# The values of an 8-head attention made in an earlier stage and kept in DRAM, and the heads' product moved one step later

## The chip, the cores and the metric

The kernel runs on one core of a Trainium2 chip. The metric is the device time of one execution in microseconds (us). All data is float32 unless said otherwise.

## The reference, cut to what matters

The input is x (32 batches of 128 tokens, 128 wide) and a context (32 x 128 tokens, 96 wide). Eight sublayers are added to x one after the other, each on a layer norm of x. Two of them matter here. The third pair's attention keeps the 32 highest of 128 scores in each of 4 heads (the "top-32 attention"). The last attention is the "8-head attention":

```python
q = (x @ Wq).reshape(B, Nq, 8, 64)
k = (context @ Wk).reshape(B, Nc, 8, 64)
v = (context @ Wv).reshape(B, Nc, 8, 64)
sim = jnp.einsum('bihd,bjhd->bhij', q, k) * 64 ** -0.5
attn = jax.nn.softmax(sim, axis=-1)
out = jnp.einsum('bhij,bjhd->bihd', attn, v)
return out.reshape(B, Nq, 512) @ Wo + bo
```

Its v depends on the context and on Wv alone, not on x.

## The kernel before, in words

The program is written for the engines by hand, stage after stage, with a barrier between stages. Within a stage each engine has its own list of instructions, in the order in which the loops write them, and semaphores tie the lists together. An instruction that waits holds up all that stands behind it on its engine.

**The film stage** (`film_in`, from about 205 to 480 us) holds the top-32 attention. It goes through the 32 batches in 16 pairs p. For each pair VectorE finds the 32 highest scores in four rounds of `max` (L1581) and `match_replace` (L1587). TensorE makes the scores of pair p+1 (L1373, L1376), turns the weights of pair p-2 (L1389), multiplies them with the context and makes the film product (L1410). ScalarE evacuates the scores from PSUM to SBUF (L1468), takes two sets of exponentials (L1452, L1460) and evacuates the film product (L1475). SP stores half of each batch's film product to DRAM (L1271) and loads the toeplitz matrices of the convolution that follows. Scores use columns 0 to 127 of PSUM banks 0 to 3.

**The 8-head stage** (`fp8_attention8`, from about 905 to 1152 us) runs steps n = -15 to 33. It has to finish two sublayers at once: the fp8 layer before (quantize x, turn it, multiply with the quantized weight, add, L2786) and the 8-head attention. Groups of four batches are prepared steps ahead: norm, turning (L2682), and per step one of the group's K products (L2623) and Q products (L2662), each 512 columns, both through PSUM bank 6. K is evacuated by ScalarE (L2720), Q by VectorE (L2825). From step 27 on no K and Q products are left. Step n then does, in this order on TensorE:

1. scores of batch n+1 (L2613, 16 listed products of two heads side by side);
2. the K product;
3. the output product of batch n-1 (L2632, bank 7), which waits for the copy `oT`;
4. the turning of batch n's weights (L2647, banks 4 and 5), which waits for GpSimd's scaling (L2581);
5. the V product of batch n+1 (L2657, bank 7);
6. the Q product;
7. the heads' product of batch n (L2670, bank 4): turned weights by values;
8. now and then four small transposes or the fp8 product: L2690 (quantized x) in steps with n mod 4 = 0, L2698 (fp8 product, bank 7) with n mod 4 = 1, L2682 (norm) with n mod 4 = 2.

ScalarE: K's evacuation, the exponentials of batch n+1, heads 0 to 3 (L2710), two evacuations of the turned weights of batch n (L2734), the exponentials of heads 4 to 7, then the evacuations and the scaling of x that belong to a group (L2747, L2753, L2759). Each exponential also gives a sum.

VectorE: the fp8 result (L2786, n mod 4 = 2), the maxima of the scores of batch n+1 (L2793), the shift, that is maximum times -1/8 (L2800, a `tensor_tensor` with both inputs in SBUF), x plus output product (L2805), the first half of a quantizing (n mod 4 = 3), the copy of V (L2819), the copy of Q (L2825), the second half of the quantizing, the moments (n mod 4 = 2), the normalizing (L2848, n mod 4 = 1), the reciprocal of the sums of batch n+1 (L2859), and the copy `oT` of the heads' product of batch n (L2864). From step 26 on the norm of the next stage is spread over five steps.

GpSimd: it waits for the reciprocal and scales the weights of batch n in two operations of 128x512 (L2581); after them stand the root of the variance (L2587 and L2589, n mod 4 = 3) and the bias added to x (L2593, n mod 4 = 2).

## Time and profile before

| | us |
|---|---|
| median of 3 runs | 1423.41 |
| lowest and highest | 1423.28 and 1425.81 |
| the profiled execution: its time | 1424.34 |
| its span, first to last instruction | 1422.6 |
| mean granted TensorE clock, share of full | 0.867 |

| engine | busy, us | share of the span |
|---|---|---|
| TensorE (PE) | 1180.1 | 83% |
| VectorE (DVE) | 986.3 | 69% |
| ScalarE (ACT) | 691.7 | 49% |
| GpSimd (POOL) | 548.6 | 39% |

A share is an average over stages with different limits, so the rows further down are read stage by stage. PE is TensorE's products, PEld its weight loads (the stationary operand), which run beside the products. A float32 product is listed as two MATMULs. In a row of the timeline the first number is the start in us from the begin of the span and the second the duration in us; "x4" means that four instructions are merged; the bracket names the idle time of the engine before the row and what ended it.

### The profile page before, as it was taken

Reading aid. Unit: us, or ns where it says so; the run is one execution under the profiler, and the core shown is the slowest. Engines: PE = TensorE matmul, PEld = TensorE weight load, DVE = VectorE, ACT = ScalarE, POOL = GpSimd, SP = SyncE. Lnnn points to the kernel's source line nnn. Section 1 sums busy time; section 2 is a strip of 40 time slices with the busy share of each in tenths; the row PEclk is TensorE's granted clock in tenths of the full one; section 3 lists DMA queues with packets and bytes.
Section 4 is the critical chain, followed back from the end, with each engine's and each line's share of the span. In section 5 each row is a group of like instructions: output and inputs, shape, how many; then the busy total and the mean of one; then the engine's idle time right before and its main releaser. Section 6 shows DMA issues by size and latency. Waiting matters only on the chain. (4 is left out here: it accounts for less than half of the span.)

```text
span 1422.6 us, 30767 instructions
## 1 busy us (share of the span) xinstructions
PE 1180.1 (83%) x10551; PEld 809.0 (57%) x10551; DVE 986.3 (69%) x3891; ACT 691.7 (49%) x2026; POOL 548.6 (39%) x770
## 2 busy tenths in 40 slices
PE   4778664767766758997899999699999989999998
PEld 3534322435444535664677777266667667776776
DVE  6767668999999269976478777676775644444433
ACT  3343245777766244432345454366666643333343
POOL 4576665677764256534133332233333310000000
PEclk8688885866676779998799999699999999898989
DMA  6400104000001411100000000000000000000000
GB/s 171 99 0 1 46 21 123 16 29 21 27 24 45 123 56 42 38 23 30 6 3 3 3 4 3 1 1 1 1 2 1 2 1 1 15 0 15 0 16 15
DMA packets 61249, 36.62 MB, mean 26 GB/s; under 512 B 19477, under 2 KB 58992, under 8 KB 61106
## 3 DMA queue, kind: packets, MB, share of 16 engines
q1 hardware_dynamic: 59802, 34.48, 8.6%
q8 instruction: 79, 1.29, 0.4%
q14 instruction: 64, 0.52, 0.1%
q10 hardware_dynamic: 1304, 0.33, 0.1%
HBM read 25.21 MB, written 6.42 MB: 22 GB/s over the span
## 5 line engine op out<-in xcount | busy, mean ns | idle before, releaser
L3037 DVE SCALAR_TENSOR_TENSOR k_X<-ps,m_gt,k_X 128x128 f32 (+1 forms) x256 | 72.0, 344 | 121.3 <-PE ps L2921 121.3
L2960 ACT ACTIVATE m_hid<-ps,k_b 128x512 f32<-128x512 f32 x128 | 81.8, 684 | 133.8 <-PE ps L2921 127.7
L2921 PEld LDWEIGHTS ps<-k_w,m_hid 128*128 128x128 f32 x1024 | 123.1, 192 | 26.8 <-issue 19.6
L2910 PE MATMUL ps<-m_xnT,k_w 128*128 128x512 f32 x256 | 128.9, 634 | 1.2 <-PEq L72 1.2
L2921 PE MATMUL ps<-k_w,m_hid 128*128 128x128 f32 x1024 | 123.3, 275 | 0.0
L2581 POOL TENSOR_TENSOR l_p<-l_p,l_rsum 128x512 f32<-128x512 f32 x64 | 65.3, 1041 | 142.8 <-DVE l_rsum L2859 142.8
L2289 DVE TENSOR_REDUCE g_peak<-ps 128x8 f32<-128x1024 f32 x64 | 75.4, 1219 | 43.5 <-PE ps L1978 43.5
L2710 ACT ACTIVATE l_p<-ps,l_shift 128x128 f32<-128x128 f32 x256 | 91.6, 391 | 19.8 <-DVE l_shift L2800 15.3
L1587 DVE MATCH_REPLACE8 v_left<-c_top,v_left 128x128 f32<-128x128 f32 x384 | 100.8, 274 | 0.0
L711 PE MATMUL ps<-f_expT,f_xeT 128*128 128x512 f32 x128 | 74.7, 718 | 27.6 <-DVE k_X L1089 27.6
L2184 ACT ACTIVATE g_pT<-ps 128x1024 f32<-128x1024 f32 x64 | 62.0, 1021 | 72.5 <-PE ps L1994 72.5
L1581 DVE MAX8 c_top<-v_left 128x8 f32<-128x128 f32 x384 | 77.9, 274 | 0.0
L121 POOL TENSOR_TENSOR m_rstd<-m_ve,k_half 128x8 f32<-128x8 f32 x4 | 6.6, 1640 | 175.6 <-DVE m_ve L114 175.6
L842 ACT ACTIVATE f_part<-ps,f_wf 128x128 f32<-128x128 f32 x128 | 36.5, 368 | 72.9 <-issue 49.1
L2910 PEld LDWEIGHTS ps<-m_xnT,k_w 128*128 128x128 f32 x256 | 48.0, 206 | 41.6 <-issue 41.6
L1389 PE MATMUL ps<-k_ident,c_exa 128*128 128x128 f32 x256 | 57.0, 414 | 10.7 <-POOL c_exa L1334 10.7
L1389 PEld LDWEIGHTS ps<-k_ident,c_exa 128*128 128x128 f32 x256 | 54.5, 321 | 18.6 <-POOL c_exa L1334 18.6
L711 PEld LDWEIGHTS ps<-f_expT,f_xeT 128*128 128x128 f32 x128 | 25.8, 225 | 65.6 <-DVE k_X L1089 44.8
L1373 PE MATMUL ps<-c_kT,c_qT 32*128 32x128 f32 x256 | 22.1, 426 | 45.3 <-ACT v_sc L1468 42.6
L1089 DVE SCALAR_TENSOR_TENSOR k_X<-ps,f_wf,k_X 128x128 f32<-128x128 f32 x128 | 44.6, 349 | 21.6 <-PE ps L711 17.5
L2710 ACT ACTIVATION_READ_ACCUMULATOR l_p<-ps,l_shift 128x1 f32 x256 | 59.1, 231 | 0.0
L1452 ACT ACTIVATE c_exb<-v_left,c_shift 128x128 f32<-128x128 f32 x128 | 49.6, 391 | 12.2 <-DVE v_left L1587 12.2
(539 smaller groups left out, 3129.9 us busy)
## 6 DMA issues: line engine op xcount, KB each, us to landing
v_toep<-kpad SPq DMA_DIRECT2D x4, 1024.0 KB, 9.2
fo_dram<-c_fo SPq DMA_DIRECT2D x32, 128.0 KB, 1.7
g_v<-fo_dram SPq DMA_DIRECT2D x8, 512.0 KB, 3.5
d_mine<-d_wad SPq DMA_DIRECT2D x32, 96.5 KB, 1.9
k_X<-in_x SPq DMA_DIRECT2D x8, 256.0 KB, 3.4
v_late<-kpad SPq DMA_DIRECT2D x2, 1024.0 KB, 8.7
out<-k_X SPq DMA_DIRECT2D x8, 256.0 KB, 2.4
f_cx<-in_ctx SPq DMA_DIRECT2D x4, 384.0 KB, 5.3
```

The lines of the kernel that those rows point to most:

```text
L711: pe.matmul(ps[:, 4 + (2 * b + h) % 3, :], xeT[:, t % 2, u, cols], expT[:, 4 * h:4 * h + 4, :].rearrange("p e d -> p (e d)"), start=True, ...
L1389: m = pe.matmul(ps[:, 4 + a, 0:128], exa[:, i % 4, h, :], k.ident[:], start=h == 0, stop=h == H - 1)
L1581: dve.max((first if r == 0 else top)[:, a, h, :], (sc if r == 0 else left)[:, i % 4, h, :]).then_inc(top_done, 1)
L1587: dve.match_replace(left[:, i % 4, h, :], (first if r == 0 else top)[:, a, h, :], (sc if r == 0 else left)[:, i % 4, h, :], TAKEN).then_in ...
L2184: act.activation(pT[:, n % 2, 2 * h:2 * h + 2, :].rearrange("p a n -> p (a n)"), ps[:, 4 + 2 * h:6 + 2 * h, :].rearrange("p a n -> p (a n) ...
L2289: dve.tensor_reduce(peak[:, (n + 1) % 2, :].rearrange("p (r c) -> p r c", r=BANDS)[:, 2 * h:2 * h + 2, 0:BANDS], ps[:, 2 * h:2 * h + 2, :] ...
L2581: pool.tensor_tensor(p[:, n % 3, 4 * a:4 * a + 4, :], p[:, n % 3, 4 * a:4 * a + 4, :], rsum[:, n % 3, 4 * a:4 * a + 4].rearrange("p (h o) ...
L2710: act.activation(p[:, i % 3, h, :], ps[:, 2 * (i % 2) + a, 128 * b:128 * b + 128], ACT.Exp, bias=shift[:, i % 2, h:h + 1], scale=SCALE, ac ...
L2910: pe.matmul(ps[:, 4 * u + q, :], k.w1_3[:, e, 128 * q:128 * q + 128], xnT[:, u], start=True, stop=True).then_inc(s["hid_ps"].sem, 1)
L2921: m = pe.matmul(ps[:, 4 * u + 2 + e % 2, j * S:j * S + S], hid[:, u, q, j * S:j * S + S], k.w2_3[:, e, q, :], start=q == 0, stop=q == 1)
L2960: act.activation(hid[:, u, q, :], ps[:, 4 * u + q, :], ACT.Gelu, bias=k.b1_3[:, 2 * e + q:2 * e + q + 1]).then_inc(s["hid"].sem, 1)
L3037: dve.scalar_tensor_tensor(out=xj[u][j], in0=ps[:, 4 * u + 2 + e % 2, j * S:j * S + S], scalar=gt[:, u, j, e:e + 1], in1=xj[u][j], op0=ALU ...
```

## The change

The V products of all batches are made in the film stage, in columns 128 to 255 of PSUM banks 0 to 3, beside the scores. TensorE makes them for batch 2p ahead of the scores of batch 2p+2, and for batch 2p+1 ahead of the scores of batch 2p+3, as four products of 128 columns each. ScalarE evacuates them (`spilled`), the one of batch 2p between the evacuation of the scores of 2p+2 and the exponentials of 2p+1, the one of 2p+1 behind the scores' of 2p+3. SP stores each as 256 KB in DRAM (`keep`). In the 8-head stage SP loads them back, three batches ahead, and the V product and its copy are gone.

In the 8-head stage, three orders change. On TensorE the heads' product of batch n-1 follows the scores of batch n+1 (it was the product of batch n at the end of the step), its result goes to bank 7, and the output product of batch n-1 stands behind the turning of batch n. On VectorE the copy `oT` of batch n-1 stands behind the shift. On ScalarE the evacuation of K stands behind the exponentials of heads 0 to 3.

```diff
@@ film_in, SP @@
+            def keep(i):
+                sp.wait_ge(val_done, i + 1)
+                sp.dma_start(k.v_dram[:, i, :], val[:, i % 2].rearrange("p h c -> p (h c)")).then_inc(k.v_out[i % 2], 16)
+
+            for i in range(4):
+                keep(i)
             for i in range(B):
...
+                if i % 2 and i + 4 < B:
+                    keep(i + 3)
+                    keep(i + 4)
@@ film_in, TensorE @@
+            def values(i):
+
+                pe.wait_ge(sc_done, min(i + 2, B))
+                if i:
+                    pe.wait_ge(val_done, i)
+                for h in range(4):
+                    m = pe.matmul(ps[:, h, 128:256], k.cT[:, S * i:S * i + S], k.wv3[:, 128 * h:128 * h + 128],
+                                  start=True, stop=True)
+                m.then_inc(val_ps, 1)
...
+                if pair(p):
+                    values(2 * p)
                 if pair(p + 1):
                     scores(2 * (p + 1))
...
+                if pair(p):
+                    values(2 * p + 1)
                 if pair(p + 1):
                     scores(2 * (p + 1) + 1)
@@ film_in, ScalarE @@
+            def spilled(i):
+                act.wait_ge(val_ps, i + 1)
+                if i >= 2:
+                    act.wait_ge(k.v_out[i % 2], 16 * (i // 2))
+                act.activation(val[:, i % 2], ps[:, 0:4, 128:256], ACT.Identity).then_inc(val_done, 1)
...
                 if pair(p + 1):
                     scored(2 * (p + 1), p)
                 if pair(p):
+                    spilled(2 * p)
+                if pair(p):
                     whole(2 * p + 1)
                 if pair(p + 1):
                     scored(2 * (p + 1) + 1, p)
+                if pair(p):
+                    spilled(2 * p + 1)
@@ fp8_attention8 @@
+        @block.sync
+        def _(sp):
+            for i in range(B):
+                if i >= 3:
+                    sp.wait_ge(av_ps, i - 2)
+                sp.dma_start(v[:, i % 3], k.v_dram[:, i, :]).then_inc(v_in[i % 3], 16)
@@ TensorE @@
+                if 0 <= n - 1 < B:
+
+                    i = n - 1
+                    pe.wait_ge(pT_done, 2 * n)
+                    pe.wait_ge(v_in[i % 3], 16 * (i // 3 + 1))
+                    pe.wait_ge(x8_done, begun(n - 1, 11))
+                    if i:
+                        pe.wait_ge(x_done, i)
+                    for b in range(4):
+                        for a in range(2):
+                            h = 2 * b + a
+                            m = pe.matmul(ps[DH * a:DH * a + DH, 7, 128 * b:128 * b + 128], v[:, i % 3, DH * h:DH * h + DH],
+                                          pT[:, i % 2, 4 * a + b, :], start=True, stop=True)
+                    m.then_inc(av_ps, 1)
                 g, b = item(n)
...
-                if 0 <= n + 1 < B:
-                    i = n + 1
-                    if n >= 1:
-                        pe.wait_ge(x_done, n)
-                    else:
-                        pe.wait_ge(v_done, i)
-                        pe.wait_ge(x8_done, begun(n - 1, 11))
-                    pe.matmul(ps[:, 7, :], k.cT[:, S * i:S * i + S], k.wv3[:], start=True, stop=True).then_inc(v_ps, 1)
+                if 0 <= n - 1 < B:
+
+                    i = n - 1
+                    pe.wait_ge(oT_done, n)
+                    for b in range(4):
+                        m = pe.matmul(ps[:, 7, 0:128], oT[:, i % 2, b, :], k.wo3[:, b, :], start=b == 0, stop=b == 3)
+                    m.then_inc(out_ps, 1)
...
@@ ScalarE @@
+                if 0 <= n + 1 < B:
+                    act.wait_ge(shift_done, n + 2)
+                    if n >= 2:
+                        act.wait_ge(pT_ps, 2 * (n - 1))
+                    weights(n + 1, 0)
                 g, b = item(n)
                 if g:
                     act.wait_ge(k_ps, 4 * g + b + 1)
                     if g >= 2 and b == 0:
                         act.wait_ge(sc_ps, G * (g - 1))
                     act.activation(kT[:, g % 2, b, :], ps[:, 6, :], ACT.Identity).then_inc(k_done, 1)
-                if 0 <= n + 1 < B:
-                    act.wait_ge(shift_done, n + 2)
-                    if n >= 2:
-                        act.wait_ge(pT_ps, 2 * (n - 1))
-                    weights(n + 1, 0)
@@ VectorE @@
                 if 0 <= n - 1 < B:
                     i = n - 1
-                    dve.wait_ge(out_ps, i + 1)
-                    dve.wait_ge(xb_done, i // G + 1)
-                    dve.scalar_tensor_tensor(out=k.X[:, i, :], in0=ps[:, 7, 0:128], scalar=k.tg[:, 3:4], in1=k.X[:, i, :],
-                                             op0=ALU.mult, op1=ALU.add).then_inc(x_done, 1)
+                    dve.wait_ge(av_ps, n)
+                    if i >= 2:
+                        dve.wait_ge(out_ps, i - 1)
+                    dve.tensor_copy(oT[:, i % 2].rearrange("p a b -> p (a b)"), ps[:, 7, :]).then_inc(oT_done, 1)
...
-                if 0 <= n + 1 < B:
-                    i = n + 1
-                    dve.wait_ge(v_ps, i + 1)
-                    if i >= 2:
-                        dve.wait_ge(av_ps, i - 1)
-                    dve.tensor_copy(v[:, i % 2], ps[:, 7, :]).then_inc(v_done, 1)
+                if 0 <= n - 1 < B:
+                    i = n - 1
+                    dve.wait_ge(out_ps, i + 1)
+                    dve.wait_ge(xb_done, i // G + 1)
+                    dve.scalar_tensor_tensor(out=k.X[:, i, :], in0=ps[:, 7, 0:128], scalar=k.tg[:, 3:4], in1=k.X[:, i, :],
+                                             op0=ALU.mult, op1=ALU.add).then_inc(x_done, 1)
...
-                if 0 <= n < B:
-                    dve.wait_ge(av_ps, n + 1)
-                    if n >= 2:
-                        dve.wait_ge(out_ps, n - 1)
-                    dve.tensor_copy(oT[:, n % 2].rearrange("p a b -> p (a b)"), ps[:, 4, :]).then_inc(oT_done, 1)
```

## Rows read from the trace of the kernel before

**Rows 1.** Busy time by stretch: top-32 attention, 8-head stage, its last steps.

```profile
core 0: us, PE busy (x) PEld busy (x) DVE busy (x) ACT busy (x) POOL busy (x), PEclk, DMA share, GB/s
300.00:360.00 60.00, 42.69 (x217) 27.51 (x216) 60.00 (x403) 43.86 (x178) 42.95 (x76) 0.67 0.08 25
1020.00:1052.00 32.00, 31.29 (x257) 21.78 (x255) 22.91 (x49) 20.78 (x82) 12.66 (x13) 1.00 0.01 2
1116.00:1145.00 29.00, 23.39 (x222) 16.98 (x221) 19.20 (x51) 17.51 (x82) 10.74 (x10) 1.00 0.01 2
```

**Rows 2.** Timeline of the 8-head stage, 1115 to 1125 us (start, duration).

```profile
1115.18 1.02 PE L2657 MATMUL ps<-k_wv,k_cT 96*128 96x512 f32 x2
...
1116.05 1.02 PE L2662 MATMUL ps<-l_xnT,k_wq 128*128 128x512 f32 x2
...
1117.11 0.69 DVE L2825 COPY l_qT<-ps 128x512 f32<-128x512 f32 x1 [0.17 <-PE ps L2662]
...
1118.49 0.18 DVE L2859 RECIPROCAL l_rsum<-l_total 128x8 f32<-128x8 f32 x1
...
1118.76 2.04 POOL L2581 TENSOR_TENSOR l_p<-l_p,l_rsum 128x512 f32<-128x512 f32 x2 [5.07 <-DVE l_rsum L2859]
...
1120.49 0.33 DVE L2800 TENSOR_TENSOR l_shift<-l_top,l_minus 128x8 f32<-128x8 f32 x1
...
1120.86 0.37 ACT L2710 ACTIVATE l_p<-ps,l_shift 128x128 f32<-128x128 f32 x1 [2.87 <-DVE l_shift L2800]
...
1122.24 1.09 ACT L2734 ACTIVATE l_pT<-ps 128x512 f32<-128x512 f32 x2
...
1124.77 0.20 DVE L2859 RECIPROCAL l_rsum<-l_total 128x8 f32<-128x8 f32 x1 [0.89 <-ACT l_p L2710]
```

**Rows 3.** Timeline, the first steps of the 8-head stage.

```profile
922.86 0.60 ACT L2720 ACTIVATE l_kT<-ps 128x512 f32<-128x512 f32 x1 [1.21 <-PE ps L2623]
...
923.35 0.36 ACT L2710 ACTIVATE l_p<-ps,l_shift 128x128 f32<-128x128 f32 x1
923.51 0.30 PEld L2662 LDWEIGHTS ps<-l_xnT,k_wq 128*128 128x128 f32 x2 [0.66 <-ACT l_kT L2720]
...
924.67 0.69 DVE L2825 COPY l_qT<-ps 128x512 f32<-128x512 f32 x1
...
926.60 0.20 DVE L2859 RECIPROCAL l_rsum<-l_total 128x8 f32<-128x8 f32 x1
...
927.92 1.02 DVE L2800 TENSOR_TENSOR l_shift<-l_top,l_minus 128x8 f32<-128x8 f32 x1
...
928.98 0.37 ACT L2710 ACTIVATE l_p<-ps,l_shift 128x128 f32<-128x128 f32 x1 [1.56 <-DVE l_shift L2800]
...
932.53 0.23 PEld L2690 LDWEIGHTS ps<-k_identb,l_xq 128*128 128x128 bf16 x4 [0.17 <-issue]
...
932.86 0.97 PEld L2613 LDWEIGHTS ps<-l_kT,l_qT 64*128 64x128 f32 x16
```

**Rows 4.** Timeline, the last reciprocal of the 8-head stage.

```profile
1143.74 0.20 DVE L2859 RECIPROCAL l_rsum<-l_total 128x8 f32<-128x8 f32 x1 [0.58 <-ACT l_p L2710]
```

**Rows 5.** Timeline, copy of Q and reciprocal in a step with moments.

```profile
1062.33 0.69 DVE L2825 COPY l_qT<-ps 128x512 f32<-128x512 f32 x1 [0.17 <-PE ps L2662]
...
1063.99 0.17 DVE L2859 RECIPROCAL l_rsum<-l_total 128x8 f32<-128x8 f32 x1
```

**Rows 6.** Timeline of the top-32 attention: second scores evacuated, first read.

```profile
364.68 0.58 ACT L1468 ACTIVATE v_sc<-ps 128x512 f32<-128x512 f32 x1
...
372.93 1.25 DVE L1581 MAX8 c_first<-v_sc 128x8 f32<-128x128 f32 x6
```

**Rows 7.** Timeline, GpSimd's root and VectorE's shift at the same time.

```profile
1037.52 1.04 POOL L2589 TENSOR_TENSOR l_rs<-l_rs,k_half 128x4 f32<-128x4 f32 x1
1037.59 0.17 DVE L2800 TENSOR_TENSOR l_shift<-l_top,l_minus 128x8 f32<-128x8 f32 x1
```

**Rows 8.** Timeline, VectorE's shift and GpSimd's bias add.

```profile
1086.78 0.42 DVE L2800 TENSOR_TENSOR l_shift<-l_top,l_minus 128x8 f32<-128x8 f32 x1
...
1087.13 1.27 POOL L2593 TENSOR_TENSOR k_X<-k_X,k_bo 128x512 f32<-128x512 f32 x1
```

More of the change, by code:

```diff
@@ L1187, in stage_film @@
         k.fo_out = [once(f"fo_out{i}") for i in range(2)]
+        k.v_out = [once(f"v_out{i}") for i in range(2)]
         k.sc = ctx.enter_context(nc.sbuf_tensor("v_sc", [128, CH, 128], F32))
@@ L1642, in _ @@
                 sp.wait_ge(k.fo_out[a], 16 * B // 2)
+                sp.wait_ge(k.v_out[a], 16 * B // 2)
         @block.tensor
@@ L2663, in _ @@
                               stop=True).then_inc(q_ps, 1)
[L2664 to L2675 removed]
+                if n == B - 1:
+                    pe.wait_ge(p_done, H * B)
+                    ex.logits(pe, ps, 0, 0)
                 g = due(n, 6)
```

41 lines of the change are left out of this document (13 added, 28 removed).

## The prediction, made before the changed kernel ran

> **What bounds the kernel now.** I read first the busy time by stretch, with the granted clock, then the 8-head stage in order of time. In 32 us of that stage TensorE is busy 31.29 us at a clock of 1.00, VectorE 22.91, ScalarE 20.78, GpSimd 12.66; in its last 29 us, where no K and Q products are left, TensorE is busy only 23.39 us, still at 1.00. In the top-32 attention VectorE is busy 60.00 of 60 us and TensorE and ScalarE 42.69 and 43.86 [rows 1]. So the change takes work from the engine that looks full and gives it to two that wait. The reader should not stop there: there is a second loop in the stage, nearly as long as TensorE's work, and it doesn't contain the product that leaves.
>
> **The second loop.** I cut steps at VectorE's reciprocal of the sums (L2859). In a last step it starts at 1118.49; GpSimd scales the weights from 1118.76 for 2.04 us, to 1120.80; the shift (L2800, VectorE, two inputs in SBUF) ends at 1120.82, and ScalarE's first exponential starts at 1120.86, 2.37 after the reciprocal. The evacuation of the turned weights follows at 1122.24, the next reciprocal at 1124.77, 3.91 after the first exponential: 6.28 in all [rows 2]. The shift waits for GpSimd, not for its maximum. The start of the stage shows it best, since no copy of the heads' product stands there between reciprocal and maximum, as none will after the change: reciprocal 926.60, shift asked for at 927.92, and it takes 1.02 instead of 0.17, so that the exponentials start at 928.98, 2.38 after the reciprocal [rows 3]. Hence the copy of the heads' product (at most the 0.69 of Q's, 1117.11) which the change moves behind the shift was free already: W, from reciprocal to first exponential, stays 2.38.
>
> **The V product** leaves TensorE's queue: 1115.18 to the Q product at 1116.05 is 0.87 a step [rows 2], its copy, 0.69 by Q's, leaves VectorE's. From first to last reciprocal, 926.60 to 1143.74, the 31 steps take 217.14 us, 7.00 each [rows 3, 4]; without V TensorE needs about 6.1 of it. If it were the only bound, 31 x 0.87 = 27 us would go.
>
> **The K evacuation** is moved on ScalarE from before the first four exponentials to behind them. Before, it ran while ScalarE waited for the shift (free). Now it stands inside the loop, between exponentials and turned weights: 922.86 to 923.35, 0.49 to 0.50 of ScalarE [rows 3]. The loop of a plain step with K and Q is 2.38 + 3.91 + 0.49 = 6.78. That is above TensorE's remaining work, so ScalarE, VectorE and GpSimd set the time.
>
> **The Q product** waits for that evacuation. Exponentials take 1120.86 to 1122.24 = 1.38, the evacuation 0.60 to its end; the load for Q follows 0.05 later, and the copy of Q starts 1.16 after that (922.86 + 0.60, 923.51, 924.67) [rows 2, 3]. So VectorE copies Q at W + 3.2 = 5.6. Behind the copy stand the norm or quantizing operations, and only then the reciprocal: 1.66 from the copy's start with moments (1062.33 to 1063.99) [rows 5], taken also for the normalizing; 1.93 with the quantizing (924.67 to 926.60) [rows 3].
>
> **Step lengths after.** A step n scales and turns batch n and takes the scores of n+1. For n mod 4, while groups are left:
> n=0: 6.78, ScalarE sets it. Here the heads' product no longer covers TensorE's wait for the copy of Q (5.6 + 0.69) ahead of the quantized transposes (932.53 to 932.86, 0.33) [rows 3], so the next scores start at 6.6 and their maximum some 1.2 later (0.97 of loads and the end of the last products, an estimate), about 1.05 after the next reciprocal. W of the next step grows by 0.2.
> n=1: 2.59 + 3.19 + 1.66 = 7.44.
> n=2: the product by the values must wait for VectorE's fp8 result (same bank); scores being early, K, turning, output product and Q queue up behind it, and the copy of Q starts 0.1 late (an estimate): 2.38 + 0.1 + 3.19 + 1.66 = 7.33.
> n=3: 2.38 + 3.19 + 1.93 = 7.50.
> The sum: 11 steps without such work 74.6, 5 of 7.44 = 37.2, 5 of 7.33 = 36.6, 4 of 7.50 = 30.0, one with a normalizing alone 7.2, one with the first of the next stage's moments 6.93 (1.38 behind the copy of Q, 1117.11 to 1118.49), and the last four as they are, 25.25 [rows 2, 4]: 217.8 against 217.14, +0.6. The step ahead of the first reciprocal adds more: its exponentials still start at 923.3, but K's evacuation ends at 925.3 instead of 923.46, and Q, its copy and the quantizing behind it shift the first reciprocal from 926.60 to 928.4, +1.8 [rows 3]. Stage: +2.4.
>
> **The top-32 side.** Each batch adds four 96x128 products and a 128x512 evacuation, 0.58 by the one of the scores (364.68). The second batch of a pair has its scores at 365.26 and VectorE asks for them at 372.93: 7.7 us of cover [rows 6]. Per pair ScalarE gets 1.2 us and TensorE about 2 (unknown: from 1.0 to 3, as the clock there is 0.67). Priced at nothing, covered by VectorE's full queue; with no cover it would be up to 16 x 3 = 48. On SP the 32 stores of 256 KB stand before stores that come a pair later, and the toeplitz loads behind them wait for later events anyway; DMA is at 8% there [rows 1]. Nothing. The loads back (three ahead, in the 8-head stage at a DMA share of 0.01) are due two steps, 13 us, after they are issued; 0, and up to +3 if the first are late. Five more semaphores have no row; taken at 0.
> The tail (last reciprocal to the experts) keeps its order share, turn, product, output: 0, between -0.5 and +0.5.
>
> **A rule weighed.** An operation of GpSimd with tiny operands does not hold the shift: L2589 runs from 1037.52 for 1.04 us, and the shift at 1037.59 takes 0.17 [rows 7]. So I charge nothing where it follows the scaling. The Trainium skill, "SBUF — State Buffer", section "SBUF: two separate sides", has GpSimd and VectorE lock their shared ports for a whole instruction, whichever starts first. By that a shift overtaken by L2589 would pay some 1.0 in each n=3 step, 5 us in all; the measured row speaks against it.
>
> **The sum**: profiled execution 1424.34 + 2.4 = 1426.7. That execution is 0.93 above the median, so for the median 1423.41 + 2.4 = **1425.8**. A measurement can tell about 0.2% (2.85 us) from no change.
>
> **Rivals.**
> *Slower, the add overtakes the shift (0.14).* In n=2 steps the bias add on GpSimd (L2593, 1.27) follows the scaling directly. After the change the shift is asked for some 0.3 before the scaling ends. It decides who gets in first. For me: the shift asked for at 1086.78, 0.4 before the scaling's end, ended at 1087.20 although the add is shown from 1087.13 [rows 8]. Against: the margin is small. If the add wins, 5 steps grow by 1.2: 1425.8 + 6 = 1432.
> *Faster, the shift slips between the two halves of the scaling (0.12).* It is asked for at 1.32 to 1.37 after the reciprocal, and the first half ends at about 1.3. At 927.92 it missed [rows 3]. Were it granted there, W falls to about 1.65, the loop to 6.05, nearly TensorE's work: 31 x 0.7, some 22 to 24 us less: 1403. If even K's evacuation were hidden, TensorE alone would bound: 1397.
> *Slower, the top-32 stage pays (0.04)*: ScalarE's 32 x 0.58 on the path: 1444.
> *Slower, TensorE's clock falls (0.03).* It idles about 1 us a step. The last steps idled as much at 1.00 [rows 1]. At the lower level its 6 us would take up to 12: tens of us, 1460 and more. The Trainium skill, "TensorE: Matmul & The Clock Gate", section "A second HAM failure mode: psum-queue depth-cycling", says that frequent small pauses between groups of products make the clock oscillate; by it this rival would hold, the rows at 1.00 do not bear it out.
> That the change does not do what it says: V's product has no other place left, so 0.
>
> **Chances.** The forecast 0.67; its own errors (W of n=1 steps, the queue behind the fp8 result, the first reciprocal) are some 2.5 us, which puts 0.25 above +2.85, 0.02 below -2.85 and 0.40 within. With the rivals: faster 0.14, same 0.40, slower 0.46. The range 1420 to 1432 takes in the add and leaves out the slipped shift, the top-32 cost and the clock. The likeliest case's own range is 1423 to 1429.
>
> **What would show it.** Right: L2657 and L2819 gone from the stage; TensorE near 27 of 32 us; reciprocal to first exponential still 2.38 with a shift of about 1 us; K's evacuation between the fourth exponential and the turned weights; plain steps of 6.78, the last four 6.28; the first reciprocal 1.8 later; VectorE 60 of 60 in the top-32 stretch. Wrong: shifts of 0.17 asked for at 1.37 (faster rival), shifts ending with L2593 (slower), idle time of VectorE before L1581, a clock under 1.00.

## The result, and the profile after

The changed kernel takes **1431.75 us** (median of 7 runs, 1429.21 to 1433.87); the kernel before 1420.81 (7 runs: the three of its table, 1423.28 to 1425.81, and four more, 1418.05 to 1420.81). The ratio is 1.0070, 95% interval 1.0053 to 1.0086: slower, by 7.5 to 12 us. The forecast was 1425.8, with 1420 to 1432 around it; the time lies 0.25 us inside the upper edge of that range and above the likeliest case's own 1423 to 1429: +10.9 us in place of +2.4.

The profiled execution after took 1431.95 us, its span is 1430.2 (1424.34 and 1422.6 before), its mean granted clock 0.882 (0.867). Stage by stage, in us of the two traces:

| stretch | before | after |
|---|---|---|
| film stage: first moments (L1577) to first Toeplitz product (L1692) | 268.6 | 274.0 |
| from there to the first maximum of the 8-head stage | 443.3 | 442.1 |
| first maximum (L2835) to first reciprocal (L2901) | 4.80 | 6.60 |
| first to last reciprocal, 31 steps | 217.1 | 222.7 |
| last reciprocal to the experts | 18.7 | 18.9 |

The rows add up to +11.7 us, while the two traces differ by 7.6: the film stage starts 2.4 us earlier in the trace after (207.4 against 209.9; 205.5 to 209.7 in all kernels with the new film stage, whose code ahead of it is the same), and from the experts on it takes 1.6 less. The stages are therefore compared one by one.

The busy time by stretch, after (the counterpart of [rows 1]; the columns are those there):

```profile
300.00:360.00 60.00, 44.76 (x279) 34.03 (x280) 60.00 (x403) 46.61 (x180) 42.42 (x77) 0.77 0.18 60
1020.00:1052.00 32.00, 28.00 (x248) 19.35 (x244) 20.85 (x46) 19.82 (x83) 11.80 (x13) 1.00 0.14 35
1121.00:1150.00 29.00, 23.96 (x220) 18.23 (x217) 18.93 (x43) 17.09 (x80) 11.78 (x11) 0.94 0.13 37
```

TensorE has fallen from 31.29 to 28.00 of 32 us, and the steps have not become shorter. VectorE still shows 60.00 of 60 us in the top-32 stretch. A plain step of the 8-head stage, after (timeline):

```profile
1120.71 0.20 DVE L2901 RECIPROCAL l_rsum<-l_total 128x8 f32<-128x8 f32 x1 [0.49 <-ACT l_p L2752]
...
1120.99 2.04 POOL L2628 TENSOR_TENSOR l_p<-l_p,l_rsum 128x512 f32<-128x512 f32 x2 [4.73 <-DVE l_rsum L2901]
...
1122.04 1.01 DVE L2842 TENSOR_TENSOR l_shift<-l_top,l_minus 128x8 f32<-128x8 f32 x1
...
1123.09 0.37 ACT L2752 ACTIVATE l_p<-ps,l_shift 128x128 f32<-128x128 f32 x1 [2.41 <-DVE l_shift L2842]
...
1124.47 0.61 ACT L2767 ACTIVATE l_kT<-ps 128x512 f32<-128x512 f32 x1
...
1124.94 1.10 ACT L2776 ACTIVATE l_pT<-ps 128x512 f32<-128x512 f32 x2
```

Reciprocal to first exponential is 2.38, with a shift of 1.01 that ends when the scaling does (1120.99 + 2.04); K's evacuation stands between the exponentials and the turned weights and takes 0.47 of the loop. In [rows 2] the turned weights followed the exponentials directly. Reciprocal to reciprocal is 6.74 to 6.77 in nearly all plain steps with K and Q (forecast 6.78) and 6.27 to 6.28 in the last four (forecast 6.28).

The first steps, TensorE's rows, after:

```profile
923.35 1.12 PE L2684 MATMUL ps<-k_cT,k_wk 96*128 96x512 f32 x2
926.97 1.13 PE L2713 MATMUL ps<-l_xnT,k_wq 128*128 128x512 f32 x2 [2.50 <-ACT l_kT L2767]
...
931.44 0.65 PE L2697 MATMUL ps<-k_ident,l_p 128*128 128x128 f32 x4 [1.19 <-POOL l_p L2628]
932.43 1.05 PE L2697 MATMUL ps<-k_ident,l_p 128*128 128x128 f32 x4 [0.34 <-POOL l_p L2628]
934.48 2.07 PE L2713 MATMUL ps<-l_xnT,k_wq 128*128 128x512 f32 x2 [1.00 <-ACT l_kT L2767]
937.39 0.58 PE L2732 MATMUL ps<-k_identb,l_xq 128*128 128x128 bf16 x4 [0.83 <-issue]
937.90 2.08 PE L2660 MATMUL ps<-l_kT,l_qT 64*128 64x128 f32 x16
```

and the granted clock there, after:

```profile
924.00:932.00 8.00, 4.31 (x26) 1.98 (x24) 5.42 (x10) 3.39 (x17) 1.73 (x3) 1.00 0.00 0
932.00:940.00 8.00, 5.83 (x29) 3.37 (x30) 1.21 (x3) 4.96 (x20) 2.41 (x3) 0.53 0.00 0
940.00:948.00 8.00, 7.35 (x56) 5.36 (x56) 4.36 (x11) 4.47 (x19) 0.02 (x1) 0.83 0.12 33
```

TensorE idles 2.50 us before the Q product of step -1, then 1.19, 0.34 and 1.00, and from 932.5 to 942.8 it is granted 1.2 instead of 2.4 GHz: the Q product takes 2.07 instead of 1.13, the scores 2.08 instead of 1.16. Steps 0 and 1 last 7.13 and 10.51 us where the same kinds last 6.76 and 7.46 later. The clock also falls in the last steps, from 1137.4 to 1140.8 (the 0.94 in the row from 1121 us), there without making a step longer.

### The profile page after: what moved, and what is told of

Its sections match the earlier page's. It is cut to its first block and busy times, and to the rows that moved or that the text cites. A ratio compares the mean times of both kernels' runs of the same rounds, so it can differ in the third digit from the quotient of the medians.

```text
span 1430.2 us, 31244 instructions
## 1 busy us (share of the span) xinstructions
PE 1176.1 (82%) x10743; PEld 829.3 (58%) x10743; DVE 973.8 (68%) x3859; ACT 706.6 (49%) x2058; POOL 549.0 (38%) x770
## 3 DMA queue, kind: packets, MB, share of 16 engines
q8 instruction: 81, 1.33, 0.4%
## 5 line engine op out<-in xcount | busy, mean ns | idle before, releaser
L711 PE MATMUL ps<-f_expT,f_xeT 128*128 128x512 f32 x128 | 70.9, 684 | 29.3 <-DVE k_X L1089 29.0
L1398 PE MATMUL ps<-k_wv,k_cT 96*128 96x128 f32 x256 | 48.0, 348 | 52.6 <-ACT c_val L1502 52.6
L1398 PEld LDWEIGHTS ps<-k_wv,k_cT 96*128 96x128 f32 x256 | 42.6, 252 | 66.1 <-ACT v_sc L1496 62.5
L1942 POOL TENSOR_TENSOR g_mq<-g_qT,g_hmask 128x512 f32<-128x512 f32 x32 | 33.2, 1039 | 56.0 <-ACT g_qT L2242 36.8
L1488 ACT ACTIVATE c_exa<-v_sc,c_shift 128x128 f32<-128x128 f32 x128 | 49.7, 398 | 5.4 <-POOL c_shift L1320 5.4
```

Source lines behind the costliest of these rows:

```text
L711: pe.matmul(ps[:, 4 + (2 * b + h) % 3, :], xeT[:, t % 2, u, cols], expT[:, 4 * h:4 * h + 4, :].rearrange("p e d -> p (e d)"), start=True, ...
L1398: m = pe.matmul(ps[:, h, 128:256], k.cT[:, S * i:S * i + S], k.wv3[:, 128 * h:128 * h + 128], start=True, stop=True)
```

## Experiments

They ran in three groups, each group on one chip beside its own runs of the kernel before (medians 1422.90, 1422.85 and 1422.23): film_only, film_nostore, k_first and filler; late_values, filler2, no_shift and old_order; the other four. Medians of different groups are compared by their ratios to before. "First to last" is the time between the first and the last reciprocal in the profiled run.

| kernel | median, us | ratio to before, 95% | film stage | first to last |
|---|---|---|---|---|
| before | | | 268.6 | 217.1 |
| changed | 1431.75 | 1.0053 to 1.0086 | 274.0 | 222.7 |
| film_only | 1425.66 | 1.0008 to 1.0030 | 274.2 | 217.1 |
| film_nostore | 1426.72 | 1.0009 to 1.0040 | 274.0 | 217.1 |
| film_products | 1422.46 | 0.9989 to 1.0006 | 268.7 | 217.1 |
| film_evac | 1423.42 | 0.9994 to 1.0022 | 268.7 | 217.1 |
| late_values | 1449.93 | 1.0174 to 1.0221 | 292.5 | 219.3 |
| filler | 1432.49 | 1.0049 to 1.0090 | 273.9 | 221.3 |
| filler2 | 1429.80 | 1.0034 to 1.0070 | 274.3 | 219.3 |
| k_first | 1423.24 | 0.9998 to 1.0027 | 274.1 | 214.7 |
| old_order | 1420.82 | 0.9969 to 0.9995 | 274.0 | 207.2 |
| no_shift | 1414.25 | 0.9922 to 0.9962 | 274.1 | 206.4 |
| old_noshift | 1408.72 | 0.9896 to 0.9924 | 274.2 | 200.0 |
| old_noshift_mf | 1436.05 | 1.0066 to 1.0123 | 274.0 | 222.5 |

### The film side

**film_only**: the changed film stage with the 8-head stage of before, which makes its own V.

> The top-32 stage of the change (V products made, evacuated, stored in DRAM), and the 8-head stage of before, which makes its own V again; the stored values are not used. Theory A (the added work in the top-32 stage costs time there): in the two traces at hand the stretch from the first moments of that stage to the first toeplitz product grew from 268.7 to 273.9 us; expected +4 to +6 us against before, VectorE's top-32 instructions at 281 ns instead of 275 and some 2 us of VectorE waiting for GpSimd's sums, and the 8-head stage as before (217 us from first to last reciprocal). Rival (VectorE's full queue covers it all, as I forecast, and the difference in the trace is from run to run): within 1.5 us of before, instructions at 275 ns.

**film_nostore**: the same without `keep` and the waits for it.

```diff
-            for i in range(4):
-                keep(i)
...
-                if i % 2 and i + 4 < B:
-                    keep(i + 3)
-                    keep(i + 4)
...
-                if i >= 2:
-                    act.wait_ge(k.v_out[i % 2], 16 * (i // 2))
```

> As film_only, but the values are not stored in DRAM (left out: the 32 stores and the waits for them; nothing reads them). Theory A1 (the stores' reads of SBUF stretch VectorE's instructions by 6 ns): instructions back at 275 ns, 2 to 3 us less than film_only. Theory A2 (it is the evacuation or the products): still 281 ns, same time as film_only within 1 us. Rival as in film_only: both within 1.5 us of before.

The film stage is 5.4 to 5.6 longer in both, and the medians rise by 2.8 and 3.8, less than theory A's 4 to 6 and more than the rival's 1.5. VectorE's top-32 instructions take 275 ns in both traces, not the 281 that theory A expected, so they are not what makes the stage longer. So the stores cost nothing, and the products and evacuations do, which the forecast had priced at nothing. In most traces part of the 5.5 is given back in the stage between, which lasts 441.5 to 442.1 us in nine of the eleven kernels with the new film stage (443.5 in late_values and 444.8 in film_only itself) and 443.3 to 443.6 in the three with the old. Why was not tried, so that the step from 5.5 in the trace to 2.8 in film_only's median stays open.

**film_products** and **film_evac** split the work of film_nostore: TensorE's products with no evacuation, and so without TensorE's waits for it (`val_done`), and ScalarE's evacuations (of the scores' columns, with one wait more ahead of the scores) with no products.

```diff
@@ film_products @@
-                if i:
-                    pe.wait_ge(val_done, i)
...
-                if pair(p):
-                    spilled(2 * p)
...
-                if pair(p):
-                    spilled(2 * p + 1)
@@ film_evac @@
-                if pair(p):
-                    values(2 * p)
...
-                if pair(p):
-                    values(2 * p + 1)
...
-                act.activation(val[:, i % 2], ps[:, 0:4, 128:256], ACT.Identity).then_inc(val_done, 1)
+                act.activation(val[:, i % 2], ps[:, 0:4, 0:128], ACT.Identity).then_inc(val_done, 1)
```

> The kernel before with the value products of the top-32 attention alone: TensorE makes them, ScalarE does not evacuate them and nothing is stored; the 8-head attention makes its own V as before, so nothing of the output is left out. It splits the film stage's cost. Theory A (TensorE's queue): what costs is that the products stand between the turning of the weights and what hangs on it; film stage 272 to 274.5 us (268.6 before, 274.0 with products and evacuation), the weights' sums late, time 1424 to 1427. Rival B (ScalarE's 1.2 us a pair): film stage 268.5 to 270, time 1422 to 1424.

> The kernel before with the evacuations of the top-32 attention alone: ScalarE copies a 128x512 block of the same banks where the values would be copied (it takes the scores, whose copy is not used), without the products; the 8-head attention makes its own V as before, so nothing of the output is left out. The other half of the split. Theory A (TensorE's queue): film stage 268.5 to 270.5 us, time 1422 to 1424. Rival B (ScalarE): 272 to 274.5, time 1424 to 1427. If both halves stay under 270.5, it takes both together.

Neither theory holds: each half alone leaves the stage at 268.7 and the time at that of before. It takes both, the case that film_evac's expectation had named. Whether it is the two amounts of work or the products' waits for the evacuations, which film_products leaves out, is not told apart. The waits of the stretch 240 to 455 us show where it goes (engine and line that waited, on what, us in total, times, longest). Before:

```profile
POOL c_share L1330 <- DVE c_share L1554: 15.8, 15, 2.8
ACT c_exb L1452 <- DVE v_left L1587: 10.7, 14, 1.2
```

film_products:

```profile
ACT v_sc L1484 <- PE ps L1380: 15.0, 14, 1.5
ACT c_exb L1468 <- DVE v_left L1607: 6.1, 7, 2.0
```

film_only:

```profile
POOL c_share L1327 <- ACT c_exb L1480: 22.0, 20, 3.2
PE ps L1398 <- ACT c_val L1502: 43.4, 14, 3.3
ACT v_sc L1496 <- PE ps L1389: 18.3, 14, 1.5
DVE c_share L1592 <- POOL c_share L1327: 2.7, 1, 2.7
ACT c_exb L1480 <- DVE v_left L1625: 0.9, 1, 0.9
```

Before, ScalarE is ahead: it waits for VectorE's last round 14 times. The products alone make it wait 15.0 us for late scores, and it still waits for VectorE 7 times; the evacuations alone bring no such wait. With both, ScalarE has its own 1.2 us a pair on top of waits for scores that stand behind products, and those behind evacuations (L1398); its exponentials of the rest (L1480) fall behind, GpSimd's sums wait for them 20 times, and once VectorE's reciprocal waits for the sums, after a pair that also brings the evacuations of K and Q. That is 2.7 us in the middle (in the traces of the changed kernel and of film_nostore it is 2.9, in three pairs); the rest, 2.7, is at the end, where last round to Toeplitz product takes 20.9 in place of 18.2 (20.3 in the changed kernel), and VectorE's wait for the sums there is 5.1 us instead of 2.8.

**late_values** tried to mend it by moving both products of a pair to just ahead of the second scores, in two column ranges, and both evacuations behind those scores.

```diff
-                if pair(p):
-                    values(2 * p)
                 if pair(p + 1):
+                    if 2 * p + 2 > 0 and pair(p - 1):
+                        pe.wait_ge(val_done, 2 * p)
                     scores(2 * (p + 1))
...
                 if pair(p):
+                    values(2 * p)
                     values(2 * p + 1)
```

> The changed kernel, but in the top-32 attention the two value products of a pair stand together in TensorE's queue just ahead of the scores of the pair's second batch (the two batches in separate column ranges of the same banks), and ScalarE evacuates both behind those scores; nothing is left out. Theory A: the values cost time there not by ScalarE's 1.2 us or TensorE's 2 us a pair but because the first product (1.91 us) stands between the turning of the weights and the product by them (L1412, L1422 of the film-only kernel), so that the weights' chain c_aT, c_exb, the sums of GpSimd and the reciprocal L1592 come some 2.7 us late, and VectorE waits (2.7 us in that trace, once) and the last batch's tail is 2 us longer. Moved, film stage 268.6 to 270 us instead of 273.9, the kernel 3.5 to 5.5 us faster than the changed one: 1426 to 1428. Rival B: what costs is the amount of work on ScalarE, 78% busy: film stage stays at 273.5 to 274.5, time 1431 to 1432.

The film stage grows to 292.5. In a bank shared with the scores the products must now wait for ScalarE's copy of the first scores (`sc_done` one higher than before), and the second scores stand behind them. VectorE's waits for the sums, late_values, 213 to 485 us:

```profile
DVE c_share L1594 <- POOL c_share L1327: 21.6, 12, 2.9
```

film_products had the products in their old place and lost nothing, so the place in TensorE's queue alone was not the cause; and my remedy, which changed waits too, made the same wait eight times as large (21.6 against 2.7).

### The start of the 8-head stage and the clock

**filler** puts two idle products of V's size ahead of the Q product of steps -1 and 0; **filler2** uses two in step -1 and in step 0 one ahead of Q's and one ahead of the turning.

```diff
@@ filler2, TensorE @@
+                if n == 0:
+                    pe.wait_ge(x8_done, begun(n - 1, 11))
+                    pe.matmul(ps[:, 7, :], k.cT[:, 0:S], k.wv3[:], start=True, stop=True)
...
+                if n in (-1, 0):
+                    pe.wait_ge(x8_done, begun(n - 1, 11))
+                    for _ in range(2 if n < 0 else 1):
+                        pe.matmul(ps[:, 7, :], k.cT[:, 0:S], k.wv3[:], start=True, stop=True)
```

> The changed kernel with two V-sized products (512 columns, result not used) put back on TensorE in steps -1 and 0, where the old V product stood and where TensorE idles in the changed kernel. Theory (TensorE's clock fell to the lower level in steps 0 and 1 because of that idle time, 0.53 between 932 and 940 us): clock 1.00 there, steps 0 and 1 take 6.8 and 7.4 instead of 7.13 and 10.51 us, 2.5 to 3.5 us less than the changed kernel. Rival (step 1 is long because the first values come late from DRAM, or for another wait): step 1 stays near 10 us, or the clock stays low.

> The changed kernel with idle V-size products (their result is not used) where TensorE waited at the start of the stage: two ahead of the Q product of step -1, and in step 0 one between K's product and the turning and one ahead of Q's. Theory A (the clock): steps 0 and 1 took 7.13 and 10.51 us instead of 6.78 and 7.46 only because TensorE, idle for 2.50, 1.19 and 1.00 us in turn, was granted 1.2 GHz from 932.5 to 942.5 us. With the gaps filled the clock stays at 1.00 from the first product on, steps 0 and 1 take 6.8 and 7.5, first to last reciprocal 219 to 219.5 instead of 222.7, time 3 to 3.5 us less than the changed kernel: 1428 to 1429. Rival B: steps 0 and 1 are long from a wait of the start (loads of V, the fp8 result), and the low clock is only its consequence: 222 to 223 whatever TensorE does, time 1432.

filler missed: steps 0 and 1 took 7.95 and 8.04, and its ratio to before is that of the changed kernel. The clock still fell, from 934.5 to 937.9, after the remaining gap of 1.20 ahead of the turning, and the idle products ran at the low level in front of Q's (timeline, filler):

```profile
932.87 0.66 PE L2697 MATMUL ps<-k_ident,l_p 128*128 128x128 f32 x4 [1.20 <-POOL l_p L2628]
...
934.37 3.52 PE L2712 MATMUL ps<-k_wv,k_cT 96*128 96x512 f32 x4
```

The kernel before has the same gap at the same place, and its clock stays at 1.00 (timeline, before):

```profile
927.98 0.66 PE L2647 MATMUL ps<-k_ident,l_p 128*128 128x128 f32 x4 [1.20 <-POOL l_p L2581]
```

filler2 has one product in that gap, and the clock holds:

```profile
924.00:932.00 8.00, 6.97 (x43) 3.78 (x43) 4.62 (x13) 4.71 (x20) 1.26 (x2) 1.00 0.00 0
932.00:940.00 8.00, 5.97 (x37) 2.95 (x37) 3.30 (x7) 4.96 (x20) 2.91 (x3) 1.00 0.00 0
```

Steps 0 and 1 are 6.76 and 7.46, first to last 219.3: in this trace theory A holds, and the clock cost the changed kernel's trace 3.4 us of the stage. The medians are less sure: against its own runs of before filler2 is 4.0 us nearer than the changed kernel, with intervals that overlap. late_values says the same without idle work. Its 8-head stage is the changed kernel's, gap of 2.50 included; there the low stretch, 947.1 to 953.9, lies mostly ahead of the first reciprocal, which comes 7.55 after the first maximum instead of 6.60, and first to last is 219.3.

### The three orders of the 8-head stage

**k_first** is the changed kernel with K's evacuation ahead of `weights(n + 1, 0)` again, as in the removed and added lines of the change, read backwards.

> The changed kernel with one order put back: on ScalarE K's evacuation stands ahead of the exponentials of heads 0 to 3 again. Theory (K's evacuation stands in the loop reciprocal, scaling, shift, exponentials): plain steps of the 8-head stage go from 6.77 to 6.28 to 6.4 us, steps with norm or quantizing get shorter by 0.3 to 0.5 as the Q product starts earlier; 10 to 16 us less than the changed kernel, so below before. The first reciprocal comes some 1.7 us earlier than with the change. Rival (TensorE's queue or the chain through the heads' product bounds the steps): under 4 us less, plain steps still above 6.6.

First reciprocal 4.80 after the first maximum, plain steps 6.28, first to last 214.7. The clock does not fall at the start of the stage, only from 1128.2 to 1131.6 in the last four steps, which stay as long as filler2's. Against filler2's 219.3 K's evacuation on the loop costs 4.6, and 1.8 at the first reciprocal. The median is 8.5 below the changed kernel's, and 10.6 when each is set against its own runs of before. Half of the theory missed: the steps with norm or quantizing did not get shorter (7.55, 7.67 and 7.43 against 7.46, 7.55 and 7.53), and the time is that of before, not below it.

The order also made the gap in which the clock fell. The Q product of step -1 waits for K's evacuation, 2.50 us in the changed kernel and 0.69 in k_first and old_order, which have no V product either. So K's evacuation behind the exponentials accounts for 4.6, 1.8 and the clock's 3.4 together.

**old_order** also takes the heads' product, its bank and its copy back to where they were before; V still comes from DRAM. Against the 8-head stage of before it is, besides SP's loads:

```diff
@@ TensorE @@
-                    pe.matmul(ps[:, 7, :], k.cT[:, S * i:S * i + S], k.wv3[:], start=True, stop=True).then_inc(v_ps, 1)
...
-                    pe.wait_ge(v_done, n + 1)
+                    pe.wait_ge(v_in[n % 3], 16 * (n // 3 + 1))
@@ VectorE @@
-                    dve.wait_ge(v_ps, i + 1)
...
-                    dve.tensor_copy(v[:, i % 2], ps[:, 7, :]).then_inc(v_done, 1)
```

> The changed kernel, but the 8-head steps in the order of before: V still comes from DRAM, the heads' product and its copy stand where they stood, K's evacuation is ahead of the exponentials. Theory A: in the order of before the second loop has neither K's evacuation nor the heads' copy in it, so that plain steps are 6.28 throughout and TensorE no longer makes any of them 6.65; first to last reciprocal 212 to 216 (217.1 before, 222.7 after), first reciprocal 4.8 after the first maximum. With the values' cost in the film stage (+5 in the traces, 2.8 in the median) the time is 1419 to 1423. Rival B: the move of the heads' product is what makes room, and without it the three long steps of a period stay as they were (7.35, 7.58, 7.85): 215.5 to 217, time 1423 to 1425.

First to last is 207.2, far below what either theory gave, while the time is within theory A's. The stage gains 9.9 on before from V's removal alone (product, copy and the waits for them), and the move of the heads' product costs 214.7 - 207.2 = 7.5. In the time only 2.0 of it is left: the film stage takes its part, and here the clock falls in the last steps, where TensorE now idles 1.88 us four times (old_order, timeline and busy time):

```profile
1129.17 1.09 PE L2710 MATMUL ps<-l_pT,l_v 128*64 128x128 f32 x16 [1.88 <-ACT l_pT L2774]
...
1135.46 1.80 PE L2710 MATMUL ps<-l_pT,l_v 128*64 128x128 f32 x16 [1.88 <-ACT l_pT L2774]
```

```profile
1136.00:1144.00 8.00, 6.47 (x39) 5.83 (x38) 1.25 (x3) 3.08 (x10) 2.04 (x2) 0.59 0.01 2
```

The tail is 21.3 instead of 18.7.

### The shift

**no_shift** is the changed kernel without the instruction that waits for GpSimd.

```diff
-                                   bias=shift[:, i % 2, h:h + 1], scale=SCALE,
+                                   bias=top[:, i % 2, h:h + 1], scale=-1.0,
...
-                    act.activation(kT[:, g % 2, b, :], ps[:, 6, :], ACT.Identity).then_inc(k_done, 1)
+                    act.activation(kT[:, g % 2, b, :], ps[:, 6, :], ACT.Identity, scale=-SCALE).then_inc(k_done, 1)
...
-                                      AX.X, ALU.max).then_inc(top_done, 1)
...
-                    dve.tensor_tensor(shift[:, a, :], top[:, a, :], minus[:], ALU.mult).then_inc(shift_done, 1)
+                                      AX.X, ALU.min).then_inc(top_done, 1)
```

> The changed kernel without the shift on VectorE: K is scaled by -1/8 as it is evacuated, the maximum becomes a minimum and is itself the bias of the exponentials, whose scale is -1. The same values up to rounding, nothing is left out but the one instruction a step. Theory A: the shift waits for GpSimd's scaling, and this wait is on the loop, so that the exponentials then start right behind the minimum, 1.35 to 1.45 us after the reciprocal instead of 2.38. A plain step falls from 6.77 to 5.8 to 6.2 (where TensorE's own work begins to set it), the four-step period from 29.3 to 26 to 27, first to last reciprocal from 222.7 to 198 to 208, the time to 1409 to 1418. Rival B: the exponentials wait for something else as well (the buffer of the weights, the scaling itself), and the wait moves from the shift to them: start still 2.3 after the reciprocal, time 1431. Rival C: TensorE is the bound already: period 28.5 to 29, time 1428.

A late plain step of no_shift (timeline):

```profile
1119.07 0.20 DVE L2895 RECIPROCAL l_rsum<-l_total 128x8 f32<-128x8 f32 x1 [0.66 <-ACT l_p L2752]
1119.19 1.17 DVE L2835 TENSOR_REDUCE l_top<-ps 128x8 f32<-128x1024 f32 x1
...
1120.40 0.37 ACT L2752 ACTIVATE l_p<-ps,l_top 128x128 f32<-128x128 f32 x1 [1.36 <-DVE l_top L2835]
```

The exponentials start 1.33 after the reciprocal, while GpSimd scales: the wait of the shift was on the loop and nothing took its place. First to last falls to 206.4, 12.9 under filler2, the same order with a steady clock (in no_shift the clock fell too, from 924.2 to 931.0, mostly ahead of the first reciprocal at 928.6, and its first step is 5.75). The time is within theory A's, but of a period's four steps only the plain one gains (6.76 to 5.72); the others are 7.74, 7.55 and 7.53 (7.46, 7.55, 7.53 in the changed kernel), and the period is 28.5 instead of 29.3, as in rival C and not theory A's 26 to 27. They have another loop, through the copy of Q. In the changed kernel, timeline from one such copy to the next:

```profile
968.36 0.69 DVE L2867 COPY l_qT<-ps 128x512 f32<-128x512 f32 x1 [1.04 <-PE ps L2713]
...
969.15 0.38 PE L2732 MATMUL ps<-k_identb,l_xq 128*128 128x128 bf16 x4 [0.83 <-issue]
969.47 1.16 PE L2660 MATMUL ps<-l_kT,l_qT 64*128 64x128 f32 x16
970.56 1.09 PE L2674 MATMUL ps<-l_pT,l_v 128*64 128x128 f32 x16
971.58 1.13 PE L2684 MATMUL ps<-k_cT,k_wk 96*128 96x512 f32 x2
972.55 1.04 PE L2697 MATMUL ps<-k_ident,l_p 128*128 128x128 f32 x8
973.42 1.06 PE L2705 MATMUL ps<-k_wo,l_oT 128*128 128x128 f32 x8
974.31 1.02 PE L2713 MATMUL ps<-l_xnT,k_wq 128*128 128x512 f32 x2
...
975.38 0.69 DVE L2867 COPY l_qT<-ps 128x512 f32<-128x512 f32 x1 [0.51 <-PE ps L2713]
```

TensorE runs without a gap from the transposes that wait for the copy of Q to the next Q product: 7.02 from copy to copy. In no_shift the same two copies stand at 1018.82 and 1025.83, 7.01. The change put the heads' product (970.56, 1.02 to the next) behind the scores, where TensorE first idles 0.83 us for the copy of Q; in old_order it starts while VectorE copies Q:

```profile
1015.40 1.02 PE L2702 MATMUL ps<-l_xnT,k_wq 128*128 128x512 f32 x2
1016.99 1.09 PE L2710 MATMUL ps<-l_pT,l_v 128*64 128x128 f32 x16 [0.57 <-ACT l_pT L2774]
```

```profile
1016.46 0.69 DVE L2859 COPY l_qT<-ps 128x512 f32<-128x512 f32 x1 [1.38 <-PE ps L2702]
```

From the copy's start to the transposes with the heads' product done takes 1.56 us in old_order (1016.46 to 1018.02) and 0.79 + 1.02 = 1.81 in the changed kernel, and the same two copies of Q stand 6.77 apart instead of 7.02. TensorE makes the same products in both orders: what the move loses is cover. k_first's period is 28.9 us, old_order's 27.5, and 1.0 of these 1.4 is TensorE idle (3.8 against 2.8 a period). k_first idles 0.83 twice for the copy of Q and 1.57 for the fp8 result, whose bank 7 the heads' product now needs; old_order idles 0.43, 0.43, 0.57 and 1.33, each time ahead of the heads' product.

**old_noshift** is old_order with the edit of no_shift; **old_noshift_mf** has the minimum ahead of the copy of the heads' product besides.

```diff
@@ old_noshift_mf, VectorE, ahead of x plus output product @@
+                if 0 <= n - 1 < B:
+                    dve.wait_ge(av_ps, n)
+                    if n >= 3:
+                        dve.wait_ge(out_ps, n - 2)
+                    dve.tensor_copy(oT[:, (n - 1) % 2].rearrange("p a b -> p (a b)"), ps[:, 4, :]).then_inc(oT_done, 1)
@@ at the end of the step @@
-                if 0 <= n < B:
...
-                    dve.tensor_copy(oT[:, n % 2].rearrange("p a b -> p (a b)"), ps[:, 4, :]).then_inc(oT_done, 1)
```

> The kernel with V from DRAM and the order of before, without the shift on VectorE (K is scaled by -1/8, the minimum is itself the bias). Theory A: with the copy of the heads' product (0.65) ahead of the minimum (1.22), the exponentials can start 2.0 us after the reciprocal instead of 2.37, so plain steps fall from 6.29 to 5.9 to 6.0 only; the steps with 6.63, 7.52 and 7.05, whose minimum waits for late scores, fall by 0 to 0.3. First to last reciprocal 207.2 to 201 to 204, time 1415 to 1418. Rival B: GpSimd's scaling, not the shift, holds the exponentials: 207, time 1420.5.

> The same, with VectorE's minimum ahead of the copy of the heads' product. Theory A: the exponentials start 1.4 us after the reciprocal, and the loop of a plain step is 1.4 + 3.9 = 5.3 us, less than TensorE's six products need (some 5.8 by their rows, turning included), so that TensorE sets the plain steps at 5.8 to 6.0. The output product, which waits for the copy, comes 1.2 later and holds the turning and the Q product behind it; that eats part of it. First to last reciprocal 197 to 203, time 1409 to 1415. Rival B: that delay outweighs the gain, since the Q product's copy sets three of four steps: longer than old_noshift, 203 to 208, time 1417 to 1421.

old_noshift is the fastest kernel of the study: 1408.72, 13.5 under before, first to last 200.0. More than its theory gave: the step that was 7.52 is 6.63, which was not expected. In that step (n mod 4 = 2) old_order's shift waits for GpSimd's bias add, and the exponentials for the shift:

```profile
972.32 1.27 POOL L2640 TENSOR_TENSOR k_X<-k_X,k_bo 128x512 f32<-128x512 f32 x1
972.63 0.98 DVE L2840 TENSOR_TENSOR l_shift<-l_top,l_minus 128x8 f32<-128x8 f32 x1
973.65 0.37 ACT L2750 ACTIVATE l_p<-ps,l_shift 128x128 f32<-128x128 f32 x1 [0.78 <-DVE l_shift L2840]
```

The kernel before has the same in its steps of 7.57: the shift takes 0.98 to 0.99 in five of the six that meet the add (0.99 at 971.86, add from 971.55). The row at 1086.78 [rows 8] is the sixth.

old_noshift_mf loses all of it (rival B, and more than it said; its six runs spread from 1428 to 1442 us). Its timeline:

```profile
1001.58 0.68 DVE L2839 COPY l_oT<-ps 128x512 f32<-128x512 f32 x1
...
1002.32 1.16 PE L2680 MATMUL ps<-k_wo,l_oT 128*128 128x128 f32 x8 [0.87 <-DVE l_oT L2839]
...
1003.31 1.04 PE L2695 MATMUL ps<-k_ident,l_p 128*128 128x128 f32 x8
...
1003.95 1.09 ACT L2774 ACTIVATE l_pT<-ps 128x512 f32<-128x512 f32 x2 [0.47 <-PE ps L2695]
```

The late copy holds the output product for 0.87 us in every step, behind it stand the turning and Q's product, and ScalarE waits for the turned weights. The clock fell here too, from 1124.8 to 1131.6, where the longest step is 8.68; what each part costs was not told apart.

## Why the prediction was right and wrong

**The account.** First to last: 217.1 before; V's product and copy gone, -9.9 (old_order); the heads' product moved, +7.5 (k_first); K's evacuation on the loop, +4.6 (filler2); the clock, +3.4 (the changed kernel): 222.7. With +1.8 ahead of the first reciprocal the stage is +7.4, and the film side adds 2.8 in the median: 10.2 of the 10.9 measured. The sum joins single traces with a median and is good to some 2 us. The forecast was +2.4 and 0.

**Inside the range by luck.** The upper end of the forecast's range, 1432, was the price of the add overtaking the shift. That did not happen, and the clock and the top-32 side, which the range left out, brought the time to 0.25 us below that end.

**Right.** The second loop, the shift that waits for GpSimd, the heads' copy free behind it, K's evacuation on the loop, the plain steps, the last four, the first reciprocal 1.8 later (6.60 against 4.80): all as written, the plain steps within 0.03 us but for two that carry moments of the next stage (7.23 for 6.93, 6.97 for 6.78). The add did not overtake the shift: with the copy `oT` behind it the shift comes ahead of the add and takes 0.35 to 0.36 in the five regular steps with the add, where it took 0.98 to 0.99 before. That gain the forecast did not name, since it went by the one row in which the shift was first. Nor did the shift slip between the two halves of the scaling, but by a small margin: in nearly all plain steps it is asked for 0.05 us after the second half (1.04) has begun, as at 1122.04 and 1121.99, and ends 0.02 after it. This agrees with the Trainium skill, "SBUF — State Buffer", section "SBUF: two separate sides", by which the instruction that starts first has the port to its end. That GpSimd's root did not hold the shift ([rows 7], and so in five steps each of the kernel before and of old_order) does not agree with it. What a shift asked for during the first half would meet no run shows.

**Right number, wrong reason.** The steps n=1 to 3 were forecast at 7.44, 7.33 and 7.50 from "2.38 (or 2.59) + 3.19 + ..." and measured 7.46, 7.55 and 7.53. That formula hangs on the shift; without the shift they did not get shorter. What sets them is TensorE's queue from one copy of Q to the next, with the moved heads' product in it. The forecast named the move only as a cover that is lost in n=0 steps and charged 0.2 to the step behind; it costs 7.5, 1.4 a period. Had the queue been followed from Q to Q, the sentence "That is above TensorE's remaining work, so ScalarE, VectorE and GpSimd set the time." would have held for the plain steps alone. In the n=2 step the fp8 result holds the product by the values until 977.82 (L2828, behind the normalizing and the reciprocal), and the copy of Q comes 0.3 late instead of 0.1: 1.1 over five steps.

**Wrong: "TensorE's clock falls (0.03)".** The step said that the last steps idled as much at 1.00 [rows 1]. They idle in pieces of some 1 us; at the stage's start the change leaves one of 2.50, with no V product and with K's evacuation behind the exponentials (0.69 in k_first). The forecast had that evacuation's delay in its first reciprocal, and not what TensorE does meanwhile. I looked for the clock in the steady steps and priced a fall of the whole stage, not one of 10 us. The Trainium skill, "TensorE: Matmul & The Clock Gate", section "A second HAM failure mode: psum-queue depth-cycling", has frequent small pauses upset the clock; in the runs here it held at 1.00 through pauses of 0.3 to 1.4 us in every steady step. It fell at the stage's start in all three kernels with a gap of 2.3 or 2.5 us there (changed, late_values, no_shift), after one of 1.20 in filler, and after four of 1.88 in old_order. But it held through the same 1.20 in the kernel before and through four of 1.62 in old_noshift, and fell for 3.4 us after 1.48 in the changed kernel's last steps. So the length of one gap does not decide alone; what does stays open.

**Wrong: the top-32 side "priced at nothing, covered by VectorE's full queue".** The cover of 7.7 us in [rows 6] is that of the scores. The exponentials of the rest have none of that kind: they start when VectorE ends a pair, and its reciprocal asks for their sums a few us later. The rival that should have been written is this one, at 3 to 5 us, not the 48 of no cover at all. That VectorE is busy 60.00 of 60 us was right in that stretch and told nothing, since its waits fall in one to three pairs late in the stage and at its end.

## What to carry to other kernels

An engine's share says nothing of a queue: follow each wait from one instance to the next (copy of Q to copy of Q), and see which instructions stand in it only by their place. A product that fills a wait costs little; moved to where the engine must first wait for something else, it is added to that wait, though the engine has room. And where work leaves TensorE at the start of a stage, look at its longest gap, not at its mean.

## What the hardware showed that was not expected

With idle products in its gaps at the stage's start TensorE stayed at 2.4 GHz (filler2), and first to last was 219.3 instead of 222.7; with none in the gap of 1.2 it fell for 3.4 us (filler, 221.3). These are single traces, and the kernel before held its clock through that gap. Products alone and evacuations alone each cost the film stage nothing (268.7 and 268.7), together 5.4. And an instruction of 0.17 us on a 128x8 tile, held 0.85 us by GpSimd in each plain step, cost 12.9 us of the stage (219.3 and 206.4): with its scale folded into K's evacuation even the new order takes 1414.25, less than the kernel before.
